# Transformer block on one Trainium2 core: maxima over all units, dense tiles opened and closed apart, v through DRAM, projections in a body's first third

## What is computed

```python
mod = (silu(c) @ wmod).reshape(8, 6, 1, 256)      # sa, ca, ga, sb, cb, gb
ga, gb = sign(g) * max(|g|, 0.25)
h = layernorm(x) * (1 + ca) + sa
q, k, v = h @ (w + b @ a / 16).T                  # LoRA folded into the weights
x = x + ga * (softmax(causal(q k^T / 4)) @ v) @ wo'.T
h = layernorm(x) * (1 + cb) + sb
w = softmax(h @ Wg.T + bg), all but the top 2 set to 0
out = x + gb * sum_e w_e * relu(h @ Wi.T + (h @ A_e.T) @ B_e.T) @ Wo.T
```

## Time and profile before

| | |
|---|---|
| median of 3 runs | 2076.18 us (2071.84 to 2076.54) |
| the profiled execution's own time | 2072.05 us |
| its span, first to last instruction | 2070.3 us |
| granted TensorE clock, mean | 0.96 |
| TensorE matmuls busy | 1851.8 us (89%) |
| VectorE busy | 1232.0 us (60%) |
| ScalarE busy | 940.3 us (45%) |
| GpSimd busy | 507.7 us (25%) |
| DMA | 111.88 MB, 103667 packets, mean 54 GB/s |

### The profile page before, as it was taken

How to read it: one execution, slowest core, us unless ns; L and a number is a source line. 1 busy time by engine, 2 the same in 40 slices (tenths; PEclk the granted TensorE clock), 3 DMA queues, 4 the chain that set the end, 5 groups by cost and what they waited for, 6 DMA issues and landing times.

```text
span 2070.3 us, 31214 instructions
## 1 busy us (share of the span) xinstructions
PE 1851.8 (89%) x10868; PEld 951.2 (46%) x10868; DVE 1232.0 (60%) x2729; ACT 940.3 (45%) x1701; POOL 507.7 (25%) x803
## 2 busy tenths in 40 slices
PE   5788987999889998899979999799988999799958
PEld 4433443445444454354634545344544545344526
DVE  5666768555774557755585556755578545764241
ACT  1255555444454445544454454544445444454320
POOL 5112211332113321223113221132211332122213
PEclk8879998999999999999999999999999999999979
DMA  4412221121211121111211122012121112110100
GB/s 134 126 42 73 63 57 32 54 68 54 62 45 54 43 86 44 37 62 57 67 32 52 57 65 60 23 56 67 59 58 51 54 65 67 32 32 11 36 0 21
DMA packets 103667, 111.88 MB, mean 54 GB/s; under 512 B 20214, under 2 KB 97618, under 8 KB 103516
## 3 DMA queue, kind: packets, MB, share of 16 engines
q1 hardware_dynamic: 103500, 109.87, 17.8%
q10 hardware_dynamic: 16, 0.02, 0.0%
HBM read 75.72 MB, written 33.58 MB: 53 GB/s over the span
## 4 chain that ended last, share of the span: by engine, by line
PE 65%; DVE 24%; ACT 5%; issue 3%; DMA 1%; SPq 1%; POOL 0%; POOLq 0%; DVEq 0%; ACTq 0%
PE dense L924 10%; PE ov L844 10%; PE st L829 8%; PE mxs L813 7%; DVE negm L1235 6%; PE dense L935 5%; DVE negm_left L1235 5%; PE dense L859 5%; PE dense L901 5%; PE dense L909 4%; PE dense L794 3%; ACT probs L983 3%; PE mxs L817 2%; DVE stats L1087 2%; DVE second L1303 1%
## 5 line engine op out<-in xcount | busy, mean ns | idle before, releaser
L983 ACT ACTIVATE probs<-st 128x512 f32<-128x512 f32 (+1 forms) x1216 | 665.4, 576 | 543.2 <-PE st L829 537.1
L1235 DVE TENSOR_REDUCE negm<-mxs 128x1 f32<-128x384 f32 (+4 forms) x736 | 431.5, 614 | 176.9 <-PE mxs L817 175.1
L829 PE MATMUL st<-q_st,k_st 98*128 98x512 bf16 (+3 forms) x1536 | 455.2, 337 | 29.0 <-ACT probs L983 14.9
L813 PE MATMUL mxs<-k_st,q_st 96*128 96x512 bf16 (+3 forms) x1280 | 400.8, 328 | 57.3 <-DVE negm L1235 33.7
L1235 DVE TENSOR_REDUCE negm_left<-mxs 128x1 f32<-128x512 f32 x512 | 334.7, 683 | 101.6 <-PE mxs L813 98.6
L844 PE MATMUL ov<-probs,v_g 128*32 128x512 f32 (+3 forms) x3072 | 337.9, 511 | 4.7 <-POOL probs L703 4.6
L813 PEld LDWEIGHTS mxs<-k_st,q_st 96*128 96x128 bf16 x1280 | 126.6, 99 | 334.3 <-DVE negm L1235 154.9
L924 PE MATMUL dense<-c_t,wi_t 128*128 128x512 f32 x512 | 245.3, 601 | 0.7 <-ACT ratio_b L1035 0.7
L700 POOL TENSOR_TENSOR fence<-fence 128x1 f32<-128x1 f32 x256 | 49.8, 194 | 736.7 <-ACT probs L983 736.5
L716 POOL TENSOR_TENSOR hid<-hid,second 128x512 f32<-128x512 f32 x128 | 160.9, 1273 | 281.3 <-DVE second L1303 281.3
L829 PEld LDWEIGHTS st<-q_st,k_st 98*128 98x128 bf16 x1536 | 142.3, 100 | 172.3 <-ACT probs L983 72.0
(11 more groups left out here) (167 smaller groups left out, 1728.3 us busy)
## 6 DMA issues: line engine op xcount, KB each, us to landing
q_st<-q_parts_scratch SPq DMA_DIRECT2D x384, 64.0 KB
k_st<-k_parts_scratch SPq DMA_DIRECT2D x384, 64.0 KB
q_parts_scratch<-q_part SPq DMA_DIRECT2D x16, 768.0 KB, 3.3
k_parts_scratch<-k_part SPq DMA_DIRECT2D x16, 768.0 KB, 4.8
xin<-in_L_attn_x SPq DMA_DIRECT2D x9, 1024.0 KB, 5.5
x<-in_L_attn_x SPq DMA_DIRECT2D x8, 1024.0 KB, 5.7
out_x<-ob SPq DMA_DIRECT2D x64, 128.0 KB, 1.7
q_st<-m_row SPq DMA_DIRECT2D x128, 4.0 KB
```

The costliest lines, as they stand in the source:

```text
L813: last = nc.tensor.matmul(mxs[:, bank_m, j * n:j * n + left], q_st[0:KS, slot, h0 + j, qt * P:(qt + 1) * P], k_st[0:KS, slot, h0 + j, k0:k ...
L829: last = nc.tensor.matmul(st[:, score_bank(ch, kt, h0), j * n:(j + 1) * n], k_st[0:KS + 2, slot, h0 + j, kt * P:(kt + 1) * P], q_st[0:KS + ...
L983: nc.scalar.activation(probs[:, par, h0:h0 + heads, 0:n], st[:, score_bank(ch, kt, h0), 0:heads * n].rearrange("p (j q) -> p j q", q=n), A ...
L1235: nc.vector.tensor_reduce(dst[:, h0:h0 + heads], src, axis=AX.X, op=ALU.max, negate=True).then_inc(max_free, 1)
```

## The change

- **Maxima** (`unit_maxima`). The 10 steps of a group's first queries (`SHORT_STEPS`) stand in k = 9, 10, 11 and 0 ahead, for the group after next, in the slot half that was read at k = 7; the other 29 in k = 1 to 8. So each unit has 2 to 4. In body 0, group 0 has all 39 in k = 0 to 8.
- **Open and close.** `pa`/`pj`, `va`/`vp`, `oa`/`op` and `fa`/`fx`/`fb` are parts of one tile, spread through a unit between maxima and scores, and an `fb` at the end of a unit goes to the start of the next. `with_banks` gives a step opened meanwhile the other bank. FFN quads are gone from the bodies (the epilogue keeps them).
- **Fixed places** in place of the planner's queue: ct 1, op 2 to 5, ls2 4 to 7, ln2 7 to 9, t2 10, rt and rx 11, ro 12 to 14, mt and rb 16; q and k tiles 0, 6, 9, 10, 11, 14, 15, 16; v tiles 7, 8, 12, 13; the 24 FFN steps one by one from 17 to 45. The next batch's ls1, ln1 and t1 stand at the end of the body before (39 to 46, `ahead`), and `xin` in unit 3. Body 0 does its own at the start (tiles from 5 to 19) and then those of the next batch. Body 6 has nothing ahead. Parts are stored by `ps` at 17 and 36.
- **v.** ScalarE copies a tile to `v_rows`, SP stores it to DRAM (`vs`) and reads a group's heads by four transfers of 64-byte pieces into `v_g` (`vg`, k = 3 in SP's order). In the prologue two v tiles stand ahead of q and k.
- **Layernorm.** `ln` 3 to 6 run on ScalarE, with one more link for the bias on VectorE. `t1` and `t2` wait for the half of the tokens that they turn.
- **Residual.** GpSimd adds what VectorE has scaled; ls2 follows add by add. x1 and the gates are loaded in halves (`xl` 0 at unit 34, `xl` 1 at the body's start).
- **Causal rows.** They go to `q_st` and `k_st` by two broadcast transfers issued by ScalarE in the prologue, in place of GpSimd's copies.

```diff
-DENSE = frozenset("su t1 pj vp ct op t2 rt rx mt rb fa wa ce nm".split())
-GOES_ON = {"fa": "fb", "wa": "w"}
+DENSE = frozenset("su t1 pa va ct oa t2 rt rx mt rb fa wa ce nm".split())
+GOES_ON = {"pa": "pj", "va": "vp", "oa": "op", "fa": "fx", "fx": "fb", "wa": "w"}
+CLOSES = frozenset(GOES_ON.values()) - frozenset(GOES_ON)
...
-VG_UNIT = 8
-V_FREE = (GROUPS - 2) * NU + VG_UNIT + 1
-V_NEEDED = (GROUPS - 1) * NU + VG_UNIT
+VG_UNIT = 2
...
+def unit_maxima(u, first_batch, lead):
+    g, k = divmod(u, NU)
+    steps = max_steps()
+    if 0 < k < LATE_MAXIMA or first_batch and g == 0 and k < LATE_MAXIMA:
+        begun = 0 if first_batch and g == 0 else SHORT_STEPS
+        group, part, i, n = g + 1, steps[begun:], k - (begun > 0), LATE_MAXIMA - (begun > 0)
+    else:
+        group, part, i, n = g + 1 + (k > 0), steps[:SHORT_STEPS], (k - LATE_MAXIMA) % NU, NU - LATE_MAXIMA + 1
+    if group >= GROUPS and not lead:
+        return []
+    return [("mx", group % 2, *s) for s in part[len(part) * i // n:len(part) * (i + 1) // n]]
...
+        slots[1] += [("ct", i) for i in range(4)]
+        for i in range(4):
+            slots[2 + i] += opened("oa", i)
+            chains[4 + i].append(("ls2", i))
+        for i, u in enumerate((7, 8, 8, 8, 9, 9, 9)):
+            chains[u].append(("ln2", i))
+        slots[10] += [("t2", i) for i in range(4)]
+        slots[11] += [("rt",), ("rx",)]
+        for i, u in enumerate((12, 12, 13, 13, 14, 14)):
+            chains[u].append(("ro", i))
+        slots[16] += [("mt", v) for v in range(2)] + [("rb", half) for half in range(2)]
+            ffn += [opened("fa", half, ft) for ft in range(8)] + [opened("wa", half, t) for t in range(4)]
+        spare = [opened(*p) for p in pj[len(PJ_UNITS):]] * pre
+        dense = ffn
+        for at, q in zip(PJ_SLOTS, spare):
+            dense = dense[:at] + [q] + dense[at:]
+        for i, q in enumerate(dense):
+            slots[17 + 30 * i // len(dense)] += q
+        if post:
+            for u, p in zip(PJ_UNITS, pj):
+                slots[u] += opened(*p)
+            for i, u in enumerate(V_UNITS):
+                slots[u] += opened("va", i)
+        else:
+            for i in range(STAT_PARTS):
+                chains[i // 2].append(("ls1", i))
+            for i in range(NORM_PARTS):
+                chains[2 + i // 4].append(("ln1", i))
+            slots[4] += [("t1", i) for i in range(4)] + [("xin",)]
+            for i, p in enumerate(pj):
+                slots[5 + 2 * i] += opened(*p)
+            for i in range(4):
+                slots[6 + 2 * i] += opened("va", i)
+        extra[PS_UNITS[0]] = ("ps", 0, 0)
+        extra[PS_UNITS[1]] = ("ps", 1, 0)
+    if ahead and post:
+        extra[3] = ("xin",)
+    if ahead:
+        for i in range(STAT_PARTS):
+            chains[39 + i // 2].append(("ls1", i))
+        for i in range(NORM_PARTS):
+            chains[41 + i // 2].append(("ln1", i))
+        slots[46] += [("t1", i) for i in range(4)]
+
...
+        together = held + slots[u]
+        held = []
+        if together and together[-1][0] == "fb" and u + 1 < GROUPS * NU:
+            held = [together.pop()]
+        begun = len([s for s in together if s[0] in ("fb", "fa")])
+        if k == 5 or k == 1 and (u > 1 or post):
+            together.insert(begun, ("ce", g, 0) if k == 5 else ("ce", (g - 1) % GROUPS, 1))
+        if k == NM_UNIT and (lead or g < GROUPS - 1):
...
+LATE_MAXIMA = 9
+SHORT_STEPS = 10
+PJ_UNITS = (0, 6, 9, 10, 11, 14, 15, 16)
+PJ_SLOTS = (5, 9, 13)
+V_UNITS = (7, 8, 12, 13)
+PS_UNITS = (17, 36)
...
-            if s[0] in GOES_ON:
-                open_at[GOES_ON[s[0]], *s[1:]] = bank
+            bank = n % 2 if n % 2 not in open_at.values() else 1 - n % 2
+            assert bank not in open_at.values() and not (open_at and needs_all(s)), (s, open_at)
+            n = bank + 1
...
+                elif kind == "vs":
+                    i = a[0]
+                    for b in range(2):
+                        after(sp, dense_free[b], done(f"vp bank{b}"))
+                    rows = v_d[done("vs") // 4 % 2].rearrange("(t p) d -> p t d", p=P)
+                    sp.dma_start(rows[:, 2 * i:2 * i + 2, :], v_rows[:, i % 2]).then_inc(v_out[i % 2], 16)
+                elif kind == "vg":
+                    g = a[0]
+                    after(sp, pv_done, done("pv") - VG_UNIT - 1)
+                    for i in range(2):
+                        sp.wait_ge(v_out[i], 16 * done(f"vs{i}"))
+                    sp.wait_ge(consts_ready, 7)
+                    rows = v_d[done("vg") // GROUPS % 2].rearrange("(t p) d -> p t d", p=P)
+                    for j in range(HG):
+                        head = slice((HG * g + j) * DH, (HG * g + j + 1) * DH)
+                        sp.dma_start(v_g[:, g % 2, :, j, 0:DH], rows[:, :, head]).then_inc(vg_in[g % 2], 16)
...
-            for stack, rows in ((q_st, q_rows), (k_st, k_rows)):
-                row_link(nc.gpsimd.tensor_copy(
-                    stack[KS:P, :, :, :].rearrange("p s j (t n) -> p (s j t) n", n=P),
-                    rows.unsqueeze(1).broadcast_to([P - KS, 2 * HG * T, P])))
-            nc.gpsimd.memset(k_st[KS:KS + 2, :, :, :], 1.0).then_inc(ones_ready, 1)
...
+                elif kind == "op":
+                    i = a[0]
+                    half = i // 2
+                    pool.wait_ge(x1_in[half], 16 * done(f"xl{half}"))
+                    pool.wait_ge(dense_free[bank], done(f"bank{bank}"))
+                    nc.gpsimd.tensor_tensor(x1[:, 2 * i:2 * i + 2, :], x1[:, 2 * i:2 * i + 2, :],
+                                            second[:, i % 2, :].rearrange("p (t d) -> p t d", t=2),
+                                            ALU.add).then_inc(x1_ready, 1)
...
+                if kind in ("ln1", "ln2"):
+                    if a[0] >= 3:
+                        src, dst, ready = (xin, xin, norm1_ready) if kind == "ln1" else (x1, x2n, norm2_ready)
+                        act.wait_ge(norm_chain, (done("normed") + 1) * NORM_LINKS)
+                        for t in range(2 * a[0] - 6, 2 * a[0] - 4):
+                            last = nc.scalar.activation(dst[:, t, :], src[:, t, :], ACT.Identity,
+                                                        scale=nt[:, 1, t:t + 1], bias=nt[:, 3, t:t + 1])
+                        last.then_inc(ready, 1)
...
+                    if a[0] == 1:
+                        act.wait_ge(rows_chain, ROW_LINKS)
+                        for i, stack in enumerate((q_st, k_st)):
+                            act.dma_start(stack[KS:P, :, :, :].rearrange("p s j (t n) -> p (s j t) n", n=P),
+                                          causal_rows[KS:P, i, :].unsqueeze(1).broadcast_to([P - KS, 2 * HG * T, P])
+                                          ).then_inc(ones_ready, 16)
...
-                    for t in range(2 * i - 6, 2 * i - 4):
-                        last = nc.vector.tensor_scalar(dst[:, t, :], src[:, t, :], mv[:, t, 0:1], y[:, t:t + 1],
-                                                       ALU.subtract, ALU.mult)
...
-                elif kind == "vg":
-                    g = a[0]
-                    if g == 0:
-                        evacuated(dve, done)
-                    after(dve, pv_done, done("pv") - VG_UNIT - 1)
-                    nc.vector.tensor_copy(
-                        v_g[:, g % 2, :, :, 0:DH],
-                        v_st[:, :, HG * DH * g:HG * DH * (g + 1)].rearrange("p t (j d) -> p t j d", j=HG)
-                    ).then_inc(vg_ready, 1)
...
-                    dve.wait_ge(dense_free[bank], done(f"bank{bank}") + 1)
-                    nc.vector.tensor_tensor(x1[:, 2 * i:2 * i + 2, :], x1[:, 2 * i:2 * i + 2, :], scaled,
-                                            ALU.add).then_inc(x1_ready, 1)
```

319 lines of the change are left out of this document (149 added, 170 removed).

## The result

The changed kernel takes **2015.83 us** (median of 4 runs, 2014.53 to 2017.08) against 2076.36 (2071.84 to 2076.65) for the kernel before, a ratio of 0.971 with a 95% interval of 0.970 to 0.973. It is faster by 60 us. The forecast of 1986 had the direction and was 30 us too low; 2015.8 lies inside the range of 1930 to 2055.

The account below looks back on a forecast made before the run. VectorE was taken to bound the first third of each body, TensorE having little else there. Five full bodies -66, body 6 -17, body 7 -9, body 0 +6, prologue -5, epilogue +1: -90, giving 1986 us; range 1930 to 2055.

Parts of the forecast that it names:

- units 5 to 8 carry 3 or 4 rather than 5: Maxima per unit once a group's 39 go over 12 units instead of 9; VectorE's excess then 6.5 us a body.
- 19.8 + 6.5 + 6.7: Losses in a full body: short losses, VectorE's excess over TensorE, late half-reads; added to 197.8 of work, 230.8 us.
- Bank waits, 0.5 to 0.7 each, 8.2 in all: Six openings close behind their bank's closing wait 0.5 to 0.7 us each; all such waits 8.2 us, before 5.5.
- the rate of 0.10: Short losses per us of TensorE's work in a body, 0.13 before in the late stretch; ends 0.07 and 0.13.
- Half-reads, 0.4, 2.2, 1.9 and 2.2: Stalls of first maxima two units after a slot's half is read again (8.9 us): 6.7 us a body, ends 0 and 13.
- VectorE from 151.6 to 141: VectorE's us in a full body, less applied layernorm 6.6, residual add 2.8, v copy 1.7, plus two links of 0.17.
- 0.55 a row: ScalarE's us for each of 16 layernorm applications of 128x256 a body, 8.8 us in all, mostly beside other work.
- Body 7: The last body, by the longest engine of each unit 195 to 185, with half a us of late reads: -9 us.
- B: Rival: spreading brings half only, as layernorm and routing chains wait on each other and banks cost 8.2: 2054 us, chance 0.23.
- A: Rival: half-reads are hidden after all, six bodies save 6.7 each and body 0 saves 8: 1938 us, chance 0.20.
- C: Rival: SP's ordered queue becomes the bound, first maxima after k = 7 and 11 held by late half-reads: 2115, chance 0.08.
- the signs named: Body 225 to 236 us, VectorE near 141, under 85% of any 25 us, clock 1.00, maxima waits under 15, statistics near 23.

Follow-up runs that it names:

- e12: The kernel before with the maxima spread over twelve units, but none in unit 9 (three units behind a half-read): 2075.3 us, ratio 1.001.
- e5: The changed kernel with an opening dense step taking the free bank idle longest, instead of the other one of the step opened last: 1971.2 us.
- e3: The changed kernel with the normalised rows of the layernorms computed on VectorE again instead of ScalarE: 2004.1 us.
- e4: The kernel before with only the maxima spread, 39 of a group over twelve units instead of nine: 2122.7 us.
- e1: The changed kernel with the maxima packed again into the first nine units of a group: 2042.3 us.

## Why the prediction was right, and where it was wrong

**Which bound.** Right that VectorE's chains with maxima stood against a TensorE at rest in the first third, and that the repair needs both sides. The step "units 5 to 8 carry 3 or 4 rather than 5" was credited with relief by itself as much as with tiles beside it; e12 shows that alone it gives nothing. No run took the tiles away from all of the first third, so the other half of the repair is read from the windows and not shown by an experiment.

**A full body: 230.8 forecast, 233.1 to 236.0 measured.** The losses were forecast as 19.8 + 6.5 + 6.7 = 33.0 us; they are 36.9 on average in bodies 1 to 5. The first third was right (69.6 us of work forecast, 69.9 counted). Three terms were not.
- *Bank waits, 0.5 to 0.7 each, 8.2 in all.* This is the term that was mis-sized. The places are right, units 18, 22, 27, 34, 38 and 42. The hidden-tile openings cost 0.4 to 0.6 each and the wa at 27 0.7; but the wa at 42 costs 2.0, because evacuation was taken as 0.9 us from the close with VectorE free, and there it is queued behind a layernorm's links. The six come to 4.8 us a body at the matmuls and 6.8 at weight loads, where six of 0.5 to 0.7 make 3.0 to 4.2. The text took them inside the rate of 0.10, as a small addition; e5 shows that they are the dearest single thing found, 44.7 us, more than the whole miss.
- *The transpose of the maxima rows*: not in the sum. It waits 2.7 us a body for m_w, at units 9 and 45, since the last maxima now fall in unit 8 and the transpose stands at the head of unit 9. The prediction asked who comes later after the spread only for the half-reads.
- *Half-reads, 0.4, 2.2, 1.9 and 2.2.* Size of one right, number of late ones wrong. At unit 33 of body 3 the issues and the wait's end are

```profile
905.50 0.62 SPq L646 DMA_DIRECT2D q_st<-blank_scratch  x1
```

```profile
914.51 0.38 PE L884 MATMUL mxs<-k_st,q_st 128*128 128x128 bf16 x4 [1.41 <-DMA k_st<-k_parts_scratch]
```

9.0 us, against 8.9 from the earlier trace rows. But TensorE's own short losses lengthen the distance as well, and the first issue goes out before the product with v from which I counted (at unit 35, 921.65 against 922.8); so only unit 33 is late, for 1.6 us a body on average and not 6.7. This error and the two before it cancel in part, and that is luck: with 1.6 for 6.7 the same sum gives 225.7 us a body, and the program would have been forecast some 31 us lower still. In body 0, forecast 8, the waits are 7.8, and with two waits for m_row (1.9) the phase came to +9.7.

**VectorE from 151.6 to 141.** Wrong: 148.9. The applied rows, the add and the copy of v are gone, as counted. But its small operations grew. The subtraction that ends m_w took, before,

```profile
L1253 DVE TENSOR_TENSOR m_w<-negm,m_w x4: 198/198/199, 813.4 to 999.5; 128x32 bf16<-128x32 f32 x4
```

and, after,

```profile
L1323 DVE TENSOR_TENSOR m_w<-negm,m_w x4: 498/502/640, 792.7 to 973.4; 128x32 bf16<-128x32 f32 x4
```

(ns, least, median and most.) One cast of low_w went from 427 to 1286 ns, one addition of the routing from 193 to 765, and the link at 955.33 above to 980 from 170, while GpSimd adds from 955.02 to 956.28. From 700 to 1250 us each of these instructions was long exactly when a GpSimd instruction was under way as it began, and then ended with it or up to 0.3 us later; in the trace of before none of them met one. The GpSimd work that they meet now is mostly old: additions to `hid`, masks, the parts of q and k. The longest subtraction for m_w, of 0.64 us, began at 792.69 beside

```profile
792.65 0.63 POOL L743 TENSOR_SCALAR_AFFINE_SELECT probs<-probs 128x512 f32<-128x512 f32 x1
```

Maxima rose from 96.2 to 99.5 us with nearly the same mean, which would fit less overlap between them; that was not isolated. The prediction took none for this contention and looked at the new residual adds alone; small operations meet it beside any GpSimd work, and now also on the way to the transpose.

**ScalarE.** 0.55 a row forecast, 0.59 measured. The price was nearly right; that the 6.6 us off VectorE buy anything was wrong (e3).

**v by transfers** cost nothing that a wait shows: TensorE never waits for v_g in the trace of the changed kernel. The loads of 64 KB land 4.0 us after issue, although in pieces of 64 bytes.

**Prologue** -6.4 for -5.3. VectorE's first statistics start at 21.94 (forecast 23, before 34.86); the two operations of 6.84 and 6.95 us are now

```profile
19.19 0.18 DVE L1150 TENSOR_SCALAR mod_t<-mod_t 128x16 f32<-128x16 f32 x1 [13.35 <-ACT k_part L1019]
19.40 0.18 DVE L1151 TENSOR_SCALAR mod_t<-mod_t 128x16 f32<-128x16 f32 x1
```

so GpSimd's copies had held them. The Trainium skill (SBUF — State Buffer, section Who interferes with whom) describes such a lock; the trace agrees, by 13.4 us here and by the m_w rows above.

**Body 7**, forecast -9, did not gain. With the bank edit it takes 201.7 us, 7.3 under before, so the term was eaten by the waits behind closings (and by half-reads, 2.9 us in all where 0.5 was forecast). **Epilogue** +3.0 for +1: 1.4 us of it by the rows on ScalarE. Between kernels with the same epilogue code this phase varied from 119.1 to 122.7, so the rest is not resolved.

**Rivals.** B (spreading brings half only, 2054) was nearest in its reasons: the chains, and banks at 8.2. A was right for three of the four half-reads, but the time that it gave was not. C did not happen in the changed kernel; its mechanism, maxima held by late half-reads, did cost 47 us in e4. Of the signs named, the full body (230.0 to 236.0) and the first statistics came out, and so did the clock, but for body 1 with 0.96 in those two tenths. VectorE's share in any 25 us (87.9% from 338.5 to 363.5, where under 85 was forecast; before, up to 97.5%), VectorE's total, the waits of maxima (16, not under 15) and the waits at units 1 and 37 did not.

## What to carry to other kernels

Before work is taken from a busy engine, or spread over it, ask what the other engine has to do beside it: here the spread brought 26 us together with the rest of the change and nothing alone (e1, e12), because the wait moved to the end of the same chain, and 6.6 us a body less on VectorE brought nothing (e3). When steps are split into openings and closings, list for each opening what closed its buffer and how long ago, and price it with the evacuating engine's queue at that place; choosing the buffer idle longest was worth 44.7 us here, where the whole change was worth 60. When one step is made later, go through all that reads its result, not the transfer alone.

## What the hardware showed that was not expected

VectorE operations on 128x8 to 128x32 elements, 0.17 to 0.20 us alone, took 0.5 to 1.0 us beside a GpSimd add or mask that reads SBUF. A link of a dependent chain can so cost as much as a pass over 128x512. Reads of 64 KB in pieces of 64 bytes landed in 4.0 us.
